# The end of each pair in the first cross-attention phase: three groups of operations in another order

## The reference

```python
xn = layernorm(x, ln_x_g, ln_x_b)          # context rows, 361 x 192
ln = layernorm(latents, ln_l_g, ln_l_b)    # the sequence's own rows, 100 x 256
q = ln @ Wq.T
kv = jnp.concatenate([xn @ Wkv.T, ln @ Wlkv.T], axis=1)   # 461 keys
qn = rmsnorm(q, qn_g) * SCALE
kn = rmsnorm(k, kn_g)
attn = jnp.einsum('bhid,bhjd->bhij', qn, kn)              # 4 heads of 64
attn = jnp.where(full_mask[:, None, None, :], attn, -jnp.finfo(attn.dtype).max)
attn = jax.nn.softmax(attn, axis=-1)
out = jnp.einsum('bhij,bhjd->bhid', attn, v)
return out @ Wo.T + bo
```

## Time and profile before

| | |
|---|---|
| median of three executions | 3698.69 us (3696.47 to 3701.03) |
| the profiled execution | 3701.03 us, span of the trace 3699.2 us |
| TensorE busy, whole span | 3483.2 us, 94% |
| DVE, ACT, POOL busy | 1922.8, 1644.2, 1560.2 us |
| granted TensorE clock, mean | 0.975 of full speed |

### The profile page before, as it was taken

The page is one execution under the profiler, slowest core; times in us unless marked ns, Lnnn a source line. Parts: engine busy times, 40 slices in busy tenths (PEclk is TensorE's granted clock), DMA queues, the critical chain, the costliest instruction groups (busy, mean ns, idle before and its releaser), DMA issues. The chain is left out here.

```text
span 3699.2 us, 71866 instructions
## 1 busy us (share of the span) xinstructions
PE 3483.2 (94%) x25820; PEld 2371.2 (64%) x25821; DVE 1922.8 (52%) x6167; ACT 1644.2 (44%) x3571; POOL 1560.2 (42%) x2142
## 2 busy tenths in 40 slices
PE   8997899998999679998899999999999989999998
PEld 5664455555666554443566666666666658899997
DVE  4654666664888655665445555545555447211114
ACT  4563455555777216776344444444444431111111
POOL 1001344444677325552455555555555547100007
PEclk9999999999999879999999999999999989999999
DMA  8401211100000351000100000000000001699973
GB/s 278 180 0 26 52 39 38 38 13 12 15 18 23 99 161 31 19 19 11 37 7 8 7 13 7 7 7 7 13 8 7 1 3 54 233 328 324 325 267 103
DMA packets 111419, 262.52 MB, mean 71 GB/s; under 512 B 24003, under 2 KB 70240, under 8 KB 95840
## 3 DMA queue, kind: packets, MB, share of 16 engines
q1 hardware_dynamic: 90208, 224.70, 19.0%
q0 software_dynamic: 16384, 26.29, 2.6%
q10 hardware_dynamic: 4608, 8.39, 0.6%
HBM read 196.61 MB, written 62.65 MB: 70 GB/s over the span
## 5 line engine op out<-in xcount | busy, mean ns | idle before, releaser
L2398 POOL TENSOR_SCALAR wide_probs<-wide_probs,wide_inverse 100x361 f32<-100x361 f32 x512 | 606.1, 1196 | 0.1
L2593 ACT ACTIVATE wide_probs<-wide_probs,wide_least 100x361 f32<-100x361 f32 x512 | 300.9, 589 | 617.2 <-DVE wide_least L2666 617.2
L2666 DVE CUSTOM_DVE_ANT_0 wide_probs<-banks,wide_bias 100x361 f32<-100x361 f32 x512 | 251.6, 529 | 218.2 <-issue 218.2
L2396 POOL TENSOR_TENSOR wide_hold_pool<-eps 100x1 f32<-100x1 f32 x256 | 50.6, 198 | 570.0 <-DVE wide_inverse L2672 569.9
L2454 PE MATMUL banks<-w_wide_v,wide_c 64*120 64x512 f32 (+1 forms) x1152 | 263.5, 590 | 2.5 <-DVE wide_v L2652 1.8
L2078 ACT ACTIVATE rot_h<-banks,w_rot_b 128x800 f32<-128x800 f32 x256 | 223.4, 924 | 86.0 <-PE banks L1952 82.7
L2448 PE MATMUL banks<-wide_c,w_wide_k 64*128 64x361 f32 x1536 | 256.0, 464 | 3.1 <-DVE wide_kT L2649 2.3
L2490 PEld LDWEIGHTS banks<-ident,wide_probs 100*120 100x120 f32 (+1 forms) x1536 | 158.3, 172 | 149.0 <-issue 118.2
L2476 PE MATMUL banks<-wide_kT,wide_qT 64*100 64x361 f32 x1024 | 221.0, 508 | 7.2 <-issue 7.2
L3097 ACT ACTIVATE tiles_hT<-banks 128x512 f32<-128x512 f32 x114 | 68.1, 597 | 348.3 <-PE banks L3013 348.3
L2672 DVE RECIPROCAL wide_inverse<-wide_rowsum 100x2 f32<-100x2 f32 x256 | 42.4, 166 | 341.6 <-ACT wide_probs L2593 341.6
(11 more groups left out here) (464 smaller groups left out, 7567.5 us busy)
## 6 DMA issues: line engine op xcount, KB each, us to landing
tiles_w<-in_moe_w SPq DMA_DIRECT2D x114, 1024.0 KB, 5.1
slots<-zeros SPq DMA_DIRECT2D x58, 512.0 KB, 5.6
cross_c<-in_ctxT SPq DMA_DIRECT2D x32, 270.8 KB, 4.4
wide_c<-in_ctxT SPq DMA_DIRECT2D x32, 270.8 KB, 4.0
mix_kT<-slots SPq DMA_DIRECT2D x32, 256.0 KB, 4.2
slots<-mix_kT ACTq DMA_DIRECT2D x32, 256.0 KB, 4.0
tiles_rows<-slots SPq DMA_DIRECT2D x57, 128.0 KB, 4.7
slots<-tiles_out SPq DMA_DIRECT2D x57, 128.0 KB, 4.9
```

Of the source, the lines that this page charges most:

```text
L2398: last = nc.gpsimd.tensor_scalar(t.probs[:, i % RING, j, :], t.probs[:, i % RING, j, :], t.inverse[:, i % RING, j:j + 1], None, ALU.mult)
L2593: last = nc.scalar.activation(t.probs[:, i % RING, j, :], t.probs[:, i % RING, j, :], ACT.Exp, bias=t.least[:, i % RING, j:j + 1], scale=-1.0,
L2666: last = nc.vector.tensor_tensor_reduce(t.probs[:, i % RING, j, :], scores(j), t.bias[:, :], -1.0, LARGEST, ALU.add, ALU.min, t.least[:, i ...
```

## The change

In three of the four `run` functions a group is moved; none is added or dropped. On TensorE `turn_probs(here, 2)` now comes before the wait for `rep[0]` and `project(before, 1)`. On ACT `weigh(here, 3)` and `keep_probs(here, 2)` come before `keep_kT(after, 0)`, and `keep_kT(after, 1)` after `keep_rows(third)`. On DVE `norm_k(after, 1, 1)` comes before `add(before, 1)`. The `run` of POOL and the loads on SP are as before.

```diff
--- before.py
+++ after.py
@@ -1423,12 +1423,12 @@
                     pe.wait_ge(s.qclip, after.n)
                 spread_sums(here, 0)
                 score(here, 3)
+                turn_probs(here, 2)
                 pe.wait_ge(rep[0], here.n)
                 if before:
                     project(before, 1)
                 if after:
                     turn_k(after, 0)
-                turn_probs(here, 2)
                 by_v(here, 1)
                 if third:
                     if before:
@@ -1536,15 +1536,14 @@
                 keep_rep(here, 0)
                 if after:
                     widen_mask(after, 0)
+                weigh(here, 3)
+                keep_probs(here, 2)
                 if after:
                     keep_kT(after, 0)
-                weigh(here, 3)
-                if after:
-                    keep_kT(after, 1)
-                keep_probs(here, 2)
                 if third:
                     keep_rows(third)
                 if after:
+                    keep_kT(after, 1)
                     widen_mask(after, 1)
 
             for lane in range(LANES):
@@ -1706,12 +1705,12 @@
                 if after:
                     norm_k(after, 1, 0)
                 mask(here, 3)
+                if after:
+                    norm_k(after, 1, 1)
                 if before:
                     add(before, 1)
                 if third:
                     rows_apply(third)
-                if after:
-                    norm_k(after, 1, 1)
                 keep_heads(here, 1)
 
             rows_stats(FIRST)
```

## The result

The changed kernel is slower: 3741.21 us, median of four (3737.97 to 3742.00), against 3697.58 (3693.62 to 3701.03, now four as well). The ratio is 1.0112, 95% interval 1.0100 to 1.0125. I had said 3722 in a range of 3714 to 3730. The direction and the stall on ACT were right, the time was not: 23 us were forecast, 43.6 came, and the clock, which I had taken at no cost, made the greater part of the difference.

A forecast was written before the change was run, and what follows sets the result against it. TensorE was taken to bound the cross phase; ACT's late K copy costs 14 x 1.49 = 20.9 us plus 2.0 in the fifteenth run, about 23 on 3698.7, giving 3722 us, range 3714 to 3730.

The forecast's parts named there:

- The bound: Cross phase: TensorE, busy 30.4 of 31.0 us per pair, bounds it; any wait for ACT or DVE is lost at once.
- (a): TensorE, turn_probs(2) moved ahead of project and turn_k(0): removes a 0.27 us wait for norm_k(1, 0), by_v(1) starts earlier.
- (b): DVE, norm_k(1, 1) ahead of rows_apply: turn_rows waits some 0.7 us, turn_k(1) 0.6 later; costed at nothing, hidden by ACT's stall.
- (c): ACT, weigh(3) and keep_probs(2) ahead of keep_kT(0): the late first K copy starts turn_k(1) 1.49 us later per pair.
- (d): ACT, keep_kT(1) behind keep_rows: not late; make_kv(0) again 1.49 us later, the next run begins with the same distances.
- The clock: TensorE's two new pauses per pair, about 0.7 and 1.0 us: granted clock stays at 1.00, no cost taken.
- Rival (D): Clock falls at each pause in the cross loop: 3.6 us per pair, 50 us more, 3772 us; chance 0.03.

The follow-up runs named there:

- control pair: The kernel before and the changed kernel, each unchanged but for a blank line, run on one chip: 3698.69 and 3738.33 us, ratio 1.0099.

## Why the prediction was wrong

- **The bound.** Right: TensorE bounds the phase and every wait shows in the period. The period went from 31.0 to 32.5 us where the clock stays up, as forecast.
- **(a), TensorE's move.** Right: by_v(1) starts 3.52 us after score(3) in place of 3.81, 0.29 earlier (0.27 forecast).
- **(b), DVE's move.** The wait of turn_rows came (0.58, 0.7 forecast), but its price alone was overestimated: 0.57 per pair, 8 us, where the two runs without ACT's move show 0.19 per pair, 2.6 us over the phase (4.2 with the fall in the tail). Two terms were too large. I had added 0.55 us for turn_rows, the step of before. That step held a wait of turn_k(1) for norm_k(1, 1), which the profile doesn't list since the ends are modelled; the bare step is 0.39 us in the run with TensorE's and DVE's moves. And the rows come 0.45 us later, not 0.61: in before the first of them starts 0.56 us behind the shift (507.14, 507.70), with TensorE's and DVE's moves 1.01. The price did not enter the sum.
- **(c) and (d), ACT's move.** Right: 1.50 against 1.49 per pair, and 23.3 us of phase against 22.9. That they agree so closely is in part luck, since each of the durations was read to some 0.05 us.
- **The clock.** This is the step that failed. "So I take no cost for it" rested on one row of the tail, a window with TensorE busy 0.52 of 1.50 us at 1.00. That one trace could not carry it: in the tail of five other traces the same wait of 1.41 or 1.48 us was followed by the lower clock. With the change such pauses, 0.58 and 1.14 us, come in fourteen pairs and one of 2.27 in the fifteenth, and behind eleven of the fifteen the clock fell to 1.2 GHz: 14.1 us. Rival (D) named the mechanism at a chance of 0.03 and priced it by the slow stretch after a wait of 7.11 us, 3.6 us per pair; a fall behind the short pause costs 1.3 us. It was given too small a chance and too high a price. The section of the Trainium skill that I had weighed and put aside ("TensorE: Matmul & The Clock Gate", "HAM oscillation — how this bites in real kernels") tells of a wait that recurs in every tile and brings the clock down each time. The trace of after agrees in that the falls recur, in eleven of fifteen pairs and not in all, with 0.72 as the granted clock of six us around such a pause.
- **The rest.** 23.3 and 14.1 make 37.4 us, the whole of the phase. The control pair on one chip differs by 39.1 in time, of which 37.4 are the phase and the other 1.7 within the scatter of the executions. In the first comparison it was 43.6; the excess of 6 us is not in the changed phase and is not there on the control's chip. Part of it is which executions are counted: with all 17 of after the difference is 41.6. What the rest was stays open.

The falls in the loop are not chance from run to run: three traces of two orders have the first ten of them in the same places, and they follow a pattern that repeats every five pairs, 547.42 to 714.70. What sets it is not settled. The falls in the tail do differ between two traces of one kernel. So the price of the clock here, eleven falls, could not have been had from the length of the pause alone; that there are falls where the pauses stand idle, and none where one is filled at the same period, is shown.

## What to carry to other kernels

Where the matrix engine is busy to 98%, a reorder that looks free must be read on the engine that hands back a buffer: here a copy moved behind two other pieces of work on ACT cost fifteen times 1.5 us. And a wait has two prices: its own length, and the clock behind it; here 1.6 or 1.7 us of pause in every pass brought it down most times, and 1.5 once in fourteen. One pause in one trace that left the clock alone says little: the same wait was followed by a fall in other traces. A filler matmul is a good probe for it, if it is judged by the length of the phase and not by the whole time.

## What the runs showed of the hardware

- Falls of the clock behind a recurring pause, in the fourteen pairs that have rows: 1.14 us idle per pair, none; 1.50, one; 1.60, eleven; 0.58 and 1.14 together, ten. Each figure is of one kernel, and the pauses also stand at other moments, so this is not a threshold.
- A single wait of one length may or may not be followed by a fall: 1.41 or 1.48 us in the tail, five of fourteen traces; 2.27 us at the fifteenth pause, both traces of the changed kernel but neither that with the first pause filled nor that with TensorE's and ACT's moves.
- With equal pauses the slow stretch began later from pair to pair and was gone in every fifth (547.42 to 714.70 in the trace of after).
- A fall cost 1.3 us here (14.1 us for eleven), and 1.5 to 1.6 in the tail.
- Three matmuls more per pass of one loop went with a second pause at the start of the passes of a later phase's loop, 1.4 and 2.1 us in place of one of 1.0 to 1.5, 25 us over that phase. With one or two more per pass that phase took 1279 and 1283 us, as without.
- One stage at the end takes 102 us on one chip and 125 on two others, with the same code.
